# A perceiver kernel on one core: six blocks of the program joined to two, and TensorE multiplies the identity while it waits

## The chip, the cores and the metric

The kernel runs on one core of a Trainium2 chip. A core has TensorE (PE, matmuls; its weight loads are PEld), VectorE (DVE), ScalarE (ACT), GpSimd (POOL) and SyncE (SP, which here only issues transfers). They run side by side and wait for each other through semaphores. The metric is device time in microseconds (us), median of several runs. The kernel before takes 1051.17 us.

## What is computed

A small sequence x of 128 rows of 256 numbers goes through two layers against a context of 12544 rows of 256 numbers. Cut to what matters:

```
# layer 0
x = x + cross_attention(layernorm(x), ctx; 4 heads of 64)        # softmax over 12544 rows
x = x + gated_delta_net(layernorm(x); 12 heads)                  # conv, silu, l2 norms, recurrence, gated norm
x = x + experts(layernorm(x); 8 experts, best 1)
# layer 1
x = layernorm(x) -> x + cross_attention(., ctx; 16 heads of 16)  # softmax over 12544 rows
x = x + gated_linear_attention(layernorm(x))                     # decay scans, sigmoid gate
x = x + experts(layernorm(x); 8 experts, best 2)
```

All matrices are float32, except the keys and queries of the second cross attention, which are split into sums of bf16 parts.

## The kernel before, in words

The program is a row of blocks. A block gives each engine its own list of instructions; between two blocks there is a barrier of all engines, and none starts the next block before every engine has ended the last. `renew` (L80) is such a barrier too, and gives semaphores back. In order of time:

1. **First block** (L298, 0 to 12.5 us): x is loaded and normalised, the queries q0 are made, and the first of 14 pieces (chunks) of the context is loaded and turned by DVE into `ctxT0`. `first_*` are this block's parts in the changed kernel.
2. **Second block** (L368, to 531 us): the loop of the first cross attention over the 14 chunks. In front of the loop stands the chunk-0 work of `PRO0`: keys (`K`, L491), the turned weights (`W`, L498 on PE, L604 and L607 on DVE), scores (`S`), keys and values for layer 1 (`J`, `V`). SP loads the weights that these need at the start of this block.
3. **Gated delta net** (one block, to 636 us), then `renew`.
4. **First experts** (`experts("moe0", ...)`, to 657 us), its own block.
5. **Second cross attention** (to 1008 us), its own block: the norm ln2, the queries, a transfer of the queries out to memory and back (L1571), 17 pairs of score matmuls for a running maximum (L1662, read by DVE at L1780), and the loop over 14 chunks (L1705 scores, L1842 exponentials on ACT, L1718 values).
6. **Linear attention** (to 1032 us), its own block: ln3, six projections (L1984), two scans on DVE, the gate (L1998), the output product (L2005), and between them the turning of the eight experts' weights (L1975).
7. **Last experts** (`experts("moe1", ...)`, to the end), its own block: norm, router (L1342), products of the experts (L1289), the sum weighted by the router on DVE (L1428), the bias.

The norm is a chain over four engines: DVE L139, L141, POOL L149, L151, DVE L144, then PE turns the result (`ln_pe`, L157) and ACT copies it to `hT` (`ln_act`, L162). PE has nothing else to do meanwhile. Each engine runs its list strictly in order, as the code is written. A float32 matmul shows as two records in the trace, a float32 transposition and a bf16 matmul as one.

Of the kernel before, what the change touches and what calls it, by code (L numbers as in the profile page):

```python
# [17 lines left out]
F32 = mybir.dt.float32  # L18
# [6 lines left out]
P = 128  # L25
# [37 lines left out]
E = 8  # L63
# [3 lines left out]
def build(nc, a, out):  # L67
# [47 lines left out]
    with ctx:  # L115
# [182 lines left out]
        with nc.Block() as block:  # L298
            @block.sync
            def _(sp):  # L300
                sp.dma_start(xres[:], a["x"].rearrange("b q d -> (b q) d")).then_inc(S("x_in"), 16)
                sp.dma_start(Wq0[:], wcols(a["L0_xattn_Wq"])).then_inc(S("wq0_in"), 16)
                load_permuted(sp, Wk0[:], a["L0_xattn_Wkv"][:, 0:D], "wk0_in")
                sp.dma_start(mask0[:, 0], mask_rows[:, 0:CH]).then_inc(S("mask0_0"), 16)

            @block.gpsimd
            def _(pool):
                pool.memset(mhalf[:], -0.5).then_inc(S("mhalf"), 1)
                pool.wait_ge(S("mhalf"), 1)
                pool.memset(ident[:], 0.0).then_inc(S("ident"), 1)  # L310
                pool.wait_ge(S("ident"), nth("ident"))
                pool.affine_select(out=ident[:], in_=ident[:], compare_op=ALU.not_equal, fill=1.0, base=0,
                                              pattern=[[-1, P]], channel_multiplier=1).then_inc(S("ident"), 1)
                pool.wait_ge(S("ident"), nth("ident"))
                ln_pool(pool, "ln0")
                pool.memset(acc0[:], 0.0).then_inc(S("acc0"), 1)
                pool.memset(run0[:], LOWEST).then_inc(S("run0_lowest"), 1)
                v = v1s[:].rearrange("p s t w -> p (s t) w")
                pool.memset(v[:, :, 0:H1 * (D1 + 1)].rearrange("p t (h d) -> p t h d", h=H1)[:, :, :, D1],
                            1.0).then_inc(S("v1_ones"), 1)  # L320
                pool.memset(v[:, :, H1 * (D1 + 1):], 0.0).then_inc(S("v1_ones"), 1)

            @block.vector
            def _(dve):
                dve.wait_ge(S("x_in"), 16)
                ln_dve(dve, "ln0")
                for k in range(4):
                    turn_context(dve, k, 0, 0, 0)
                dve.wait_ge(S("q0_psum"), 1)
                dve.tensor_scalar(q0[:].rearrange("p b q -> p (b q)"), bank[1][:, 0:D], S0, None,  # L330
                                  ALU.mult).then_inc(S("q0"), 1)

            @block.tensor
            def _(pe):
                pe.wait_ge(S("ident"), 2)
                ln_pe(pe, "ln0", 0)
                pe.wait_ge(S("ln0_hT"), 1)
                pe.wait_ge(S("wq0_in"), 16)
                for b in range(DC):
                    for k in range(DC):  # L340
                        ins = pe.matmul(bank[1][:, b * P:(b + 1) * P], Wq0[:, k, b * P:(b + 1) * P], hT[:, k, :],
                                        start=(k == 0), stop=(k == DC - 1))
                ins.then_inc(S("q0_psum"), 1)

            @block.scalar
            def _(act):
                load_context(act, 0, 0)
                ln_act(act, "ln0", 0)
# [19 lines left out]
        with nc.Block() as block:  # L368
            @block.gpsimd
            def _(pool):  # L370
                pool.tensor_copy(identb[:], ident[:]).then_inc(S("identb"), 1)
# [54 lines left out]
            def _(sp):  # L426
                def load(c, s):
# [46 lines left out]
            def _(pe):  # L474
                def kv_free(op, c):
# [105 lines left out]
            def _(dve):  # L581
                def side(op, c, s, n):
# [82 lines left out]
            def _(act):  # L665
                def side(op, c, s, n):
# [134 lines left out]
        with nc.Block() as block:  # L801
# [287 lines left out]
            def _(pe):  # L1089
# [51 lines left out]

                pe.wait_ge(S("o0"), 1)
# [118 lines left out]
        def experts(tag, router, router_rows, router_bias, expert_bias, top, last, loads=None, clears=None, turned=None):  # L1261
# [31 lines left out]
            with nc.Block() as block:  # L1293
                @block.sync
# [740 lines left out]
```

## Time and profile before

| | |
|---|---|
| median of 3 runs | 1051.17 us (1048.46 to 1052.52) |
| the profiled execution | 1051.36 us, its span 1049.6 us |
| PE busy | 970.8 us, 92% of the span |
| DVE, ACT, POOL busy | 494.8, 536.3, 301.9 us |
| mean granted clock of TensorE | 0.954 of full |

### The profile page before, as it was taken

The page shows a single profiled execution, that of the slowest core. Times are in us where ns is not written, and L with a number is a line of the kernel's source. Part 1 is how long each engine was busy: PE and PEld are TensorE (multiplying, and loading weights), DVE is VectorE, ACT ScalarE, POOL GpSimd, SP SyncE. Part 2 cuts the span into 40 slices and gives each one's busy share as a digit, 9 for nine tenths or more (in the row PEclk, how much of TensorE's full clock was granted, in tenths as well). Part 3 has the DMA queues.
Part 4 walks back from the last instruction along what each step waited for, and adds up shares of the span by engine and source line. Part 5 has one row for each costly group of instructions (what it writes and reads, how often), then busy time and mean ns, then how long its engine had stood idle before and what let it go on. Part 6 is the DMA issues. An engine that isn't in the chain of part 4 may idle for free. (4 is left out here: it accounts for less than half of the span.)

```text
span 1049.6 us, 21941 instructions
## 1 busy us (share of the span) xinstructions
PE 970.8 (92%) x8332; PEld 582.6 (56%) x8332; DVE 494.8 (47%) x1002; ACT 536.3 (51%) x1250; POOL 301.9 (29%) x424
## 2 busy tenths in 40 slices
PE   6999999999999999999978888589999999999967
PEld 3444544554554445455457875236667666666754
DVE  3224233332423232242245462478778887787434
ACT  1544544454455445455537732126667666666742
POOL 4543353444435344443502710610110000100000
PEclk9999999999999999999979997659999999999987
DMA  6466547535565544443210005676556776566000
GB/s 135 149 176 184 174 171 187 141 141 104 127 182 181 140 128 148 95 124 144 99 46 1 2 2 135 167 192 174 154 148 180 176 191 185 147 164 189 25 1 6
DMA packets 106060, 136.78 MB, mean 130 GB/s; under 512 B 66568, under 2 KB 87840, under 8 KB 103296
## 3 DMA queue, kind: packets, MB, share of 16 engines
q1 hardware_dynamic: 102272, 134.81, 46.5%
q10 hardware_dynamic: 3712, 0.92, 0.6%
q8 instruction: 53, 0.87, 0.3%
q14 instruction: 23, 0.19, 0.1%
HBM read 81.88 MB, written 53.26 MB: 129 GB/s over the span
## 5 line engine op out<-in xcount | busy, mean ns | idle before, releaser
L1780 DVE TENSOR_REDUCE mx<-bank 128x1 f32<-128x896 f32 x224 | 234.1, 1086 | 60.6 <-PE bank L1662 57.6
L1842 ACT ACTIVATE p<-bank 128x512 f32<-128x512 f32 x392 | 204.2, 601 | 105.3 <-PE bank L1705 105.1
L526 PE MATMUL bank<-Wv,ctxT 128*128 128x512 f32 x392 | 183.6, 603 | 0.0
L1662 PE MATMUL bank<-krows,qrows 96*128 96x512 bf16 x448 | 132.0, 379 | 11.2 <-DMA qrows<-qscr 6.7
L1705 PE MATMUL bank<-qrows,krows 99*128 99x128 bf16 x1568 | 125.6, 222 | 5.3 <-ACT p L1842 4.9
L1705 PEld LDWEIGHTS bank<-qrows,krows 99*128 99x128 bf16 x1568 | 100.6, 98 | 42.9 <-issue 10.5
L594 DVE CUSTOM_DVE_ANT_0 sc<-bank,pen 128x448 f32<-128x448 f32 x112 | 65.7, 620 | 102.9 <-issue 102.9
L1718 PE MATMUL bank<-p,v 128*32 128x128 f32 x3136 | 108.5, 277 | 5.1 <-issue 5.1
L413 POOL CAST kt<-kf 128x512 bf16<-128x512 f32 (+1 forms) x56 | 31.2, 558 | 278.4 <-ACT kf L685 278.4
L526 PEld LDWEIGHTS bank<-Wv,ctxT 128*128 128x128 f32 x392 | 70.1, 190 | 72.9 <-issue 68.6
L1718 PEld LDWEIGHTS bank<-p,v 128*32 128x32 f32 x3136 | 80.8, 110 | 39.4 <-ACT p L1842 31.5
L696 ACT COPY v<-bank 128x256 f32<-128x256 f32 x98 | 36.3, 370 | 116.5 <-PE bank L526 116.5
L507 PE MATMUL bank<-ctxT,WTk 128*128 128x512 f32 (+1 forms) x224 | 95.0, 547 | 0.4 <-ACT v1s L697 0.4
L491 PE MATMUL bank<-ctxT,Wk 128*128 128x448 f32 x224 | 90.6, 549 | 3.0 <-PEq L298 3.0
L1601 POOL TENSOR_SCALAR neg<-run 128x16 f32<-128x16 f32 x14 | 3.6, 256 | 271.6 <-DVE run L1795 271.6
L717 ACT COPY pT<-bank 128x512 f32<-128x512 f32 x98 | 56.6, 583 | 47.2 <-PE bank L537 47.1
L709 ACT ACTIVATE sc<-sc,neg 128x448 f32<-128x448 f32 x112 | 73.5, 663 | 0.0
L685 ACT ACTIVATE kf<-bank,b 128x512 f32<-128x512 f32 (+1 forms) x56 | 35.5, 634 | 67.5 <-PE bank L507 67.5
L620 DVE COPY ots<-bank 128x256 f32<-128x256 f32 x14 | 5.9, 425 | 131.4 <-PE bank L549 131.4
L537 PE MATMUL bank<-ident,sc 128*128 128x128 f32 x392 | 62.3, 282 | 4.0 <-ACT pT L717 1.7
L537 PEld LDWEIGHTS bank<-ident,sc 128*128 128x128 f32 x392 | 42.8, 140 | 40.0 <-issue 31.8
L507 PEld LDWEIGHTS bank<-ctxT,WTk 128*128 128x128 f32 x224 | 40.2, 190 | 44.8 <-issue 23.2
(285 smaller groups left out, 1200.7 us busy)
## 6 DMA issues: line engine op xcount, KB each, us to landing
krows<-kscr SPq DMA_DIRECT2D x14, 1536.0 KB, 9.6
krows<-kscr SPq DMA_DIRECT2D x14, 1152.0 KB, 14.3
vscr<-v1s SPq DMA_DIRECT2D x14, 1004.5 KB, 3.9
v<-vscr SPq DMA_DIRECT2D x14, 1004.5 KB, 12.5
ctx<-ctx SPq DMA_DIRECT2D x104, 112.0 KB, 3.6
kscr<-kt SPq DMA_DIRECT2D x14, 768.0 KB, 3.6
kscr<-kt SPq DMA_DIRECT2D x14, 576.0 KB, 3.0
kscr<-kt SPq DMA_DIRECT2D x14, 512.0 KB, 4.5
```

The costliest lines, as they stand in the source:

```text
L491: ins = pe.matmul(bank[kv_bank(op, s)][:, 0:HCH], Wk0[:, i, b * P:(b + 1) * P], ctxT0[:, i, half * HCH:(half + 1) * HCH], start=(i == 0), ...
L507: ins = pe.matmul(bank[kv_bank(op, s)][:, 0:HW[half]], WTk[:, i, b * P:(b + 1) * P], ctxT0[:, i, HO[half]:HO[half] + HW[half]], start=(i = ...
L526: ins = pe.matmul(bank[kv_bank(op, s)][:], ctxT0[:, i, k * P:(k + 1) * P], Wv01[:, i].rearrange("p w o -> p (w o)"), start=(i == 0), stop= ...
L537: ins = pe.transpose(bank[PT[(s + t) % 2]][:, h * P:(h + 1) * P], sc0[:, s, h, t * P:(t + 1) * P], ident[:])
L594: dve.tensor_tensor_reduce(out=sc0[:, s, h, half * HCH:(half + 1) * HCH], in0=bank[SX[k % 2]][:, 0:HCH], in1=pen0[:, half * HCH:(half + 1) ...
L709: act.activation(sc0[:, s, h, cols], sc0[:, s, h, cols], ACT.Exp, bias=neg0[:, h:h + 1], accum_out=den0[:, s, h, half:half + 1]).then_inc( ...
L717: act.copy(pT0[:, t % NPT, :], bank[PT[(s + t) % 2]][:]).then_inc(S("pT0"), 1)
L1662: ins = pe.matmul(bank[b + half][:, 0:HW[half]], qrows[0:KROWS, 0, h, :], krows[half][0:KROWS, r, krow(h), :], start=True, stop=True)
L1705: ins = pe.matmul(bank[ST1[g % 3]][:, i * P:(i + 1) * P], krows[half][:, c % R1, krow(h), cols], qrows[:, c % 2, h, :], start=True, stop=True)
L1718: ins = pe.matmul(bank[OT1][32 * i:32 * i + 32, j * P:(j + 1) * P], v1[:, c % R1, t, h * (D1 + 1):h * (D1 + 1) + 32], p1[:, g % PR, i * P: ...
L1780: dve.tensor_reduce(mx1[:, c % 2, h:h + 1], psum[:, b:b + 2, :].rearrange("p b n -> p (b n)")[:, 0:CH], AX.X, ALU.max).then_inc(S("smread1 ...
L1842: act.activation(p1[:, g % PR, :], bank[ST1[g % 3]][:], ACT.Exp).then_inc(S("exp1"), 1)
```

## The change

**Blocks joined.** The first two blocks become one, and the last four (first experts, second cross attention, linear attention, last experts) become one. Each engine's lists are put one behind the other: `first_tensor(pe)` and then the second block's list, and `moe0[3](pe)`, `second_tensor(pe)`, `linear_tensor(pe)`, `moe1[3](pe)`. Where a barrier had stood for an order between engines, three waits are written: VectorE waits for `run0_lowest` ahead of the first running maximum and for the last rescaling of `acc1` ahead of the linear attention, SP for `ln3_xn` ahead of the last experts' small loads. q0 is made in bank 7 instead of bank 1. The barrier at `renew` and that behind the first attention's loop stay.

**Products of the identity.** A helper `spin(pe, b, n)` multiplies the 128x128 float32 identity with itself n times into a bank that nothing reads. It is called at 20 places, 119 products in all (`spin` counts below), nearly all just ahead of a place where PE waits for a norm, a softmax or a copy.

```diff
+        def spin(pe, b, n):
+            for _ in range(n):
+                pe.matmul(bank[b][:, 0:P], ident[:], ident[:], start=True, stop=True)
...
+        def first_tensor(pe):
+            pe.wait_ge(S("ident"), 2)
+            spin(pe, OT, 9)
+            ln_pe(pe, "ln0", 0)
+            spin(pe, OT, 3)
+            pe.wait_ge(S("ln0_hT"), 1)
...
+            ins.then_inc(S("q0_psum"), 1)
+            spin(pe, OT, 3)
...
                 penalty(0, 0, 0)
+                dve.wait_ge(S("run0_lowest"), 1)
...
+                spin(pe, 5, 5)
                 pe.wait_ge(S("o0"), 1)
...
                 ins.then_inc(S("x1_psum"), 1)
+                spin(pe, 5, 11)
                 ln_pe(pe, "ln1", 7)
+                spin(pe, 5, 2)
                 pe.wait_ge(S("ln1_hT"), 1)
...
                 pe.wait_ge(S("masks"), MASKS)
+                pe.wait_ge(S("qcopy"), 2)
+                spin(pe, 2, 14)
                 pe.wait_ge(S("sq"), 1)
                 norms(ZB[0], 0, "n2k")
-                pe.wait_ge(S("qcopy"), 2)
...
+                spin(pe, 6, 11)
                 for g in range(NG):
                     pe.wait_ge(S("on"), g + 1)
                     heads(g, ZB[g], lambda h: oh[:, h], None, "oT_psum", True)
+                    if g == 0:
+                        spin(pe, 6, 6)
...
+                if last:
+                    pe.wait_ge(S(n("eT")), 5)
+                spin(pe, 3 if last else 7, 6 if last else 3)
+                ln_pe(pe, n("ln"), 0)
+                spin(pe, 3 if last else 7, 2)
...
+            spin(pe, 3, 10)
+            ln_pe(pe, "ln2", 4)
+            spin(pe, 3, 2)
...
+            for n, op in enumerate(PRO1):
+                side(*op)
+            if n >= len(PRO1) - 6:
+                spin(pe, OT1, 2)
...
+        def linear_vector(dve):
+            dve.wait_ge(S("acc1"), 2 * NCH + 1)
...
+        def linear_tensor(pe):
+            spin(pe, 6, 9)
+            ln_pe(pe, "ln3", 0)
+            spin(pe, 6, 2)
...
+            expert(0)
+            expert(1)
+            spin(pe, 6, 7)
+            pe.wait_ge(S("qs"), DC)
...
+            expert(2)
+            expert(3)
+            spin(pe, 6, 10)
+            pe.wait_ge(S("ol"), 1)
...
         with nc.Block() as block:
+            @block.sync
+            def _(sp):
+                moe0[1](sp)
+                second_sync(sp)
+                sp.wait_ge(S("ln3_xn"), 1)
+                moe1[1](sp)
...
+            @block.tensor
+            def _(pe):
+                moe0[3](pe)
+                second_tensor(pe)
+                linear_tensor(pe)
+                moe1[3](pe)
```

The order of instructions at three places, before and now. First PE at the start of the program, before (`ctxT,Wk` are the first keys, L298 and L473 the end of one block and the entry of the next):

```order
L157 MATMUL bank<-ident,xn 128x128 x2
L341 MATMUL bank<-hT,Wq 128x128 x4
L298 UNCONDITIONAL_BRANCH
L473 UNCONDITIONAL_BRANCH
L491 MATMUL bank<-ctxT,Wk 128x448 x8
L498 MATMUL bank<-ident,v 128x128 x4
L518 MATMUL bank<-kT,q 128x448 x2
```

and now:

```order
L163 MATMUL bank<-ident 128x128 x9
L157 MATMUL bank<-ident,xn 128x128 x2
L163 MATMUL bank<-ident 128x128 x3
L343 MATMUL bank<-hT,Wq 128x128 x4
L163 MATMUL bank<-ident 128x128 x3
L496 MATMUL bank<-ctxT,Wk 128x448 x8
L503 MATMUL bank<-ident,v 128x128 x4
L523 MATMUL bank<-kT,q 128x448 x2
L512 MATMUL bank<-ctxT,WTk 128x512 x2
```

The end of the block between the queries (L341, now L343) and the keys is gone, and 15 products stand around the norm and the queries.

Then SP, the queue of transfers, at the same place, before (`v<-` with L_xattn_Wk, Wv and Wq are the weights of layer 1, loaded into the space of `v0`; `Wv` is the weight of the values):

```order
L301 DMA xres<-x 128x256
L302 DMA Wq<-L_xattn_Wq 128x2x256
L296 DMA Wk<-L_xattn_Wkv 32x2x256 x4
L304 DMA mask<-mask_BxSxS_bf 128x896
L298 UNCONDITIONAL_BRANCH
L425 UNCONDITIONAL_BRANCH
L271 DMA v<-L_xattn_Wk 32x8x64 x4
L271 DMA v<-L_xattn_Wv 32x8x64 x4
L450 DMA v<-L_xattn_Wq 128x2x256
L296 DMA Wv<-L_xattn_Wkv 32x2x256 x4
```

and now:

```order
L304 DMA xres<-x 128x256
L305 DMA Wq<-L_xattn_Wq 128x2x256
L301 DMA Wk<-L_xattn_Wkv 32x2x256 x4
L307 DMA mask<-mask_BxSxS_bf 128x896
L276 DMA v<-L_xattn_Wk 32x8x64 x4
L276 DMA v<-L_xattn_Wv 32x8x64 x4
L454 DMA v<-L_xattn_Wq 128x2x256
L301 DMA Wv<-L_xattn_Wkv 32x2x256 x4
```

The weights of layer 1 stand directly behind the mask, without the end of the block between them.

Last PE from the end of the second attention into the linear attention, before (`ident,ots` is the last turn of values, L1984 the projections, L1975 the turned experts' weights, L1991 the divisor, L1998 the gate):

```order
L1679 MATMUL bank<-ident,ots 128x128 x4
L1551 UNCONDITIONAL_BRANCH
L1967 UNCONDITIONAL_BRANCH
L157 MATMUL bank<-ident,xn 128x128 x2
L1984 MATMUL bank<-hT,lT 128x128 x12
L1975 MATMUL bank<-ident,ew 128x128 x8
L1991 MATMUL bank<-qs,blk 128x256
L1975 MATMUL bank<-ident,ew 128x128 x8
L1998 MATMUL bank<-ol,lT 128x128 x4
L1975 MATMUL bank<-ident,ew 128x128 x8
L2005 MATMUL bank<-lT,kvp 128x256 x2
L1975 MATMUL bank<-ident,ew 128x128 x8
```

and now:

```order
L1690 MATMUL bank<-ident,ots 128x128 x4
L163 MATMUL bank<-ident 128x128 x9
L157 MATMUL bank<-ident,xn 128x128 x2
L163 MATMUL bank<-ident 128x128 x2
L1996 MATMUL bank<-hT,lT 128x128 x12
L1985 MATMUL bank<-ident,ew 128x128 x8
L163 MATMUL bank<-ident 128x128 x7
L2004 MATMUL bank<-qs,blk 128x256
L1985 MATMUL bank<-ident,ew 128x128 x8
L163 MATMUL bank<-ident 128x128 x10
L2012 MATMUL bank<-ol,lT 128x128 x4
L1985 MATMUL bank<-ident,ew 128x128 x8
```

Nine products stand in the place of the end of the block, and two, seven and ten more ahead of the three places at which PE waits.

## Rows read from the trace of the kernel before

**Rows 1.** Page, part 2: granted clock in tenths, 40 slices of the span.

```profile
PEclk9999999999999999999979997659999999999987
```

**Rows 2.** Windows: length; busy us (records) of PE, PEld, DVE, ACT, POOL; PEclk; DMA; GB/s.

```profile
1008.00:1010.00 2.00, 0.00 (x0) 0.00 (x0) 1.71 (x5) 0.00 (x0) 0.00 (x0) 1.00 0.03 8
1011.00:1016.90 5.90, 4.89 (x21) 4.49 (x22) 1.22 (x5) 0.37 (x1) 0.00 (x0) 0.50 0.00 0
639.00:648.00 9.00, 7.99 (x26) 5.29 (x26) 2.78 (x13) 4.17 (x8) 1.45 (x5) 0.50 0.59 181
```

**Rows 3.** Timeline: start us, length us, engine, line, operation; first block and after.

```profile
3.62 0.43 SPq L304 DMA_DIRECT2D mask<-mask_BxSxS_bf  x1
...
7.88 2.08 PE L341 MATMUL bank<-hT,Wq 128*128 128x128 f32 x8 [1.31 <-ACT hT L162]
...
11.00 1.17 DVE L285 STREAM_TRANSPOSE ctxT<-ctx 128x448 f32<-128x448 f32 x2 [2.10 <-DMA ctx<-ctx]
...
12.76 1.79 SPq L271 DMA_DIRECT2D v<-L_xattn_Wk  x4
...
12.98 8.16 PE L491 MATMUL bank<-ctxT,Wk 128*128 128x448 f32 x16 [3.02 <-PEq L298]
...
19.81 0.64 DVE L604 STREAM_TRANSPOSE WTk<-v 128x128 f32<-128x128 f32 x2 [6.27 <-DMA v<-L_xattn_Wq]
```

**Rows 4.** Timeline of the steady loop and of the second stage, clock at full.

```profile
46.62 3.17 PE L491 MATMUL bank<-ctxT,Wk 128*128 128x448 f32 x8
...
571.35 1.95 PE L1105 MATMUL bank<-hT,Wc 128*128 128x128 f32 x16
```

**Rows 5.** Timeline of the second stage, first half.

```profile
533.91 2.07 PE L1149 MATMUL bank<-Wo,oT 128*128 128x256 f32 x4 [0.46 <-ACT oT L1020]
...
546.28 5.31 DVE L887 SCALAR_TENSOR_TENSOR cv<-xpad,convw,cv 128x128 f32<-128x128 f32 x18 [0.38 <-ACT cv L978]
...
553.18 1.47 PE L1119 MATMUL bank<-half,sq 128*128 128x2 f32 x12 [1.80 <-DVE sq L896]
```

**Rows 6.** Timeline of the second stage, end.

```profile
628.80 3.10 PE L1138 MATMUL bank<-Wo,oT 128*128 128x256 f32 x8
...
632.17 3.62 PE L1138 MATMUL bank<-Wo,oT 128*128 128x256 f32 x16
```

**Rows 7.** Timeline of the first mixture of experts.

```profile
638.32 1.94 PE L1325 MATMUL bank<-ident,ew 128*128 128x128 f32 x8 [2.53 <-PEq L83]
...
644.85 3.60 PE L1289 MATMUL bank<-eTmoe,hT 128*128 128x512 f32 x4
...
649.16 1.88 PE L1289 MATMUL bank<-eTmoe,hT 128*128 128x512 f32 x4
```

**Rows 8.** Timeline of the second attention, ahead of its loop.

```profile
657.55 0.43 DVE L139 BATCH_NORM_STATS2 stats<-xres 128x6 f32<-128x256 f32 x1 [0.53 <-PEq L1293]
...
660.88 2.07 PE L1728 MATMUL bank<-hT,WTq 128*128 128x128 f32 x8 [0.46 <-ACT hT L162]
...
703.67 1.09 DVE L1780 TENSOR_REDUCE mx<-bank 128x1 f32<-128x896 f32 x1 [2.35 <-PE bank L1662]
```

**Rows 9.** Timeline of the linear attention and the last mixture.

```profile
1011.55 0.69 PE L157 MATMUL bank<-ident,xn 128*128 128x128 f32 x2 [4.26 <-DVE xn L144]
...
1012.70 4.95 PE L1984 MATMUL bank<-hT,lT 128*128 128x128 f32 x24 [0.46 <-ACT hT L162]
...
1024.46 2.08 PE L1998 MATMUL bank<-ol,lT 128*128 128x128 f32 x8 [2.71 <-DVE ol L1932]
...
1028.24 2.08 PE L2005 MATMUL bank<-lT,kvp 128*128 128x256 f32 x4
...
1032.36 0.43 DVE L139 BATCH_NORM_STATS2 stats<-xres 128x6 f32<-128x256 f32 x1 [1.59 <-PEq L1883]
...
1036.64 9.19 PE L1289 MATMUL bank<-eT,hT 128*128 128x512 f32 x16
```

**Rows 10.** Waits of VectorE, 1006 to 1050 us: us, times, longest.

```profile
DVE xres L1428 <- PE bank L1289: 1.8, 3, 0.7
```

More of the change, by code:

```diff
@@ L296, in load_permuted @@
                 sp.dma_start(tile[j * SQ:(j + 1) * SQ], rows[j]).then_inc(S(name), 16)
[L298 to L348, printed above, removed]
@@ L352, in kv_bank, with first_scalar @@
+        def first_scalar(act):
+            load_context(act, 0, 0)
+            ln_act(act, "ln0", 0)
         def kv_bank(op, s):
@@ new lines, in mixture_scalar, with expert @@
+            def mixture_scalar(act):
+                def expert(i):
+                    act.wait_ge(S(n("eT_psum")), i + 1)
+                    act.copy(eT[:, :, i, :], bank[3 + i % 2][:].rearrange("p (k o) -> p k o", k=DC)
+                             ).then_inc(S(n("eT")), 1)
+                if not last:
+                    expert(0)
+                    expert(1)
+                if router_rows:
+                    act.wait_ge(S(n("rwT_psum")), 1)
+                    act.copy(rwT[:].rearrange("p k e -> p (k e)"), bank[1][:, 0:DC * E]).then_inc(S(n("rwT")), 1)
+                ln_act(act, n("ln"), 0)
+                for i in range(2, E):
+                    if not last:
+                        expert(i)
+                    if i == 2:
+                        act.wait_ge(S(n("shifted")), 1)
+                        act.activation(ex[:], lx[:], ACT.Exp).then_inc(S(n("ex")), 1)
+                act.wait_ge(S(n("wtT_psum")), 1)
+                act.copy(wtT[:], bank[1][0:E, 0:P]).then_inc(S(n("wtT")), 1)
@@ L1501, in build @@
         renew(("ew0_in",))
-        experts("moe0", a["L0_ffn_router_w"], True, a["L0_ffn_router_b"], a["L0_ffn_expert_b"], 1, False,
+        moe0 = experts("moe0", a["L0_ffn_router_w"], True, a["L0_ffn_router_b"], a["L0_ffn_expert_b"], 1, False,
                 l1_loads, l1_clears)
@@ L1866, in build @@
+        moe0[0].close()
         l1.close()
@@ new lines, in linear_scalar, with expert @@
+        def linear_scalar(act):
+            def expert(i):
+                act.wait_ge(S("moe1eT_psum"), i + 1)
+                act.copy(eT1[:, :, i, :], bank[EB[i % 4]][:].rearrange("p (k o) -> p k o", k=DC)).then_inc(S("moe1eT"), 1)
+            ln_act(act, "ln3", 0)
+            act.wait_ge(S("ng"), 1)
+            act.activation(ng[:], ng[:], ACT.Exp).then_inc(S("eng"), 1)
+            act.wait_ge(S("qkv_psum"), 2)
+            act.copy(qkv[:, 4:6], bank[4][:, 0:D].rearrange("p (c t) -> p c t", c=2)).then_inc(S("vl"), 1)
+            expert(0)
+            expert(1)
+            act.activation(spare[:], bg[:, 0:1], ACT.Sigmoid)
+            expert(2)
+            act.wait_ge(S("gate_psum"), 1)
+            for c in range(DC):
+                act.activation(gl[:, c], bank[6][:, c * P:(c + 1) * P], ACT.Sigmoid,
+                               bias=bg[:, c:c + 1]).then_inc(S("gate"), 1)
+            for i in range(3, E):
+                expert(i)
@@ L1884, in _ @@
+        moe1 = experts("moe1", a["L1_ffn_Wg"], False, a["L1_ffn_bg"], a["L1_ffn_be"], 2, True, turned=eT1)
+        with nc.Block() as block:
+            @block.sync
[4 more added lines that the diff above has]
+                moe1[1](sp)
             @block.gpsimd
             def _(pool):
-                ln_pool(pool, "ln3")
+                moe0[2](pool)
+                second_gpsimd(pool)
+                linear_gpsimd(pool)
+                moe1[2](pool)
+            @block.tensor
[4 more added lines that the diff above has]
+                moe1[3](pe)
+            @block.scalar
+            def _(act):
+                moe0[4](act)
+                second_scalar(act)
+                linear_scalar(act)
+                moe1[4](act)
@@ L2010, in build @@
-        experts("moe1", a["L1_ffn_Wg"], False, a["L1_ffn_bg"], a["L1_ffn_be"], 2, True, turned=eT1)
+                moe0[5](dve)
+                second_vector(dve)
+                linear_vector(dve)
+                moe1[5](dve)
+        moe1[0].close()
         la.close()
```

1024 lines of the change are left out of this document (501 added, 523 removed).

## The prediction, made before the changed kernel was run

> **What bounds the kernel now.** I read the page first. PE is busy in nearly the whole span, but the slices of the granted clock are not all 9: there are dips behind the middle and at the end [rows 1]. So I cut the span at the stages and asked for the granted clock of short windows. It has two levels, 1.00 (2.4 GHz) and 0.50 (1.2 GHz). From 1008 to 1010 us PE has no record and the clock is still 1.00; from 1011 to 1016.9 us it works through at 0.50; from 639 to 648 us likewise [rows 2]. Each fall comes behind a stretch in which PE did little, and the work behind the wait pays for it. The timelines of the small stages then show what ends each wait. These stages are one chain over four engines; every microsecond saved on it is a microsecond of the kernel, and the two loops only move forward.
>
> **The unit.** At full clock 16 records of 128 columns take 1.95 us [rows 4], 0.12 each. At 0.50, 8 records take 2.08 us [rows 9]; 8 at full would take 8 x 0.12 + 0.1 for the end = 1.07. So 1024 columns of float32 records cost 1.0 us more at the low level. In the first block the clock column reads full, but the 8 records of the queries took the same 2.08 us [rows 3], so I take them as low. A product of the identity is two such records: 0.24 us at full, 0.5 at low.
>
> **Start.** Before, the queries end at 7.88 + 2.08 = 9.96, and the keys start at 12.98 because the block has to end; they take 8.16 us [rows 3] where the same 16 records take 2 x 3.17 = 6.34 in the loop [rows 4]. The first half of the context is turned long before, the second at 11.00 + 1.17 = 12.17 [rows 3]. Now nine products fill PE until the norm comes, three the copy, so that the queries or at the latest the keys run at full clock: queries until 8.9, three products until 9.7, the first half of the keys until 12.8, later than 12.17, the rest until 16.0. Before it was 21.14: 5.1 us earlier at best. The next work needs the turned weights of layer 1, whose transfers were issued from 12.76 and awaited until 19.81. SP now issues them behind the mask, from 3.62 + 0.43 = 4.05, 8.7 us earlier [rows 3]; they have 16.0 - (19.81 - 8.7) = 4.9 us of slack to share the engines with the context. I take 4.3, since the first products run low and may be 0.4 us too long at two places. Bounds: 5.1 above; below, 1.0, the queries' clock alone, if sharing costs the transfers all that the earlier issue gives.
>
> The Trainium skill (DMA: Bandwidth & Descriptors, Issuing engines are not separate DMA queues) says that transfers from different engines run on the same 16 DMA engines and interleave. By that rule the weights on SP's queue delay the context on ACT's, which this trace cannot show, since before nothing followed the mask on SP. It is the third rival below.
>
> **Delta net, first half.** Five products stand ahead of the turn of o0, eleven in the norm, two at the copy. They keep the clock: the output product of 4 records of 256 columns goes from 2.07 to 1.05 [rows 5], the two turns save 0.2 each, the gate projection (4 records) about 0.5. These 1.9 us reach VectorE's chain to R. Behind R the convolutions waited 0.38 us more for ACT's taps, which waited for PE [rows 5]; at full clock PE is early, so this goes too. Sum 2.3. Bounds 1.0 (the clock falls once) and 2.5. Fourteen products (3.4 us) stand ahead of the norms, where PE waited 1.80 us [rows 5]. They fit because PE's projections ahead of them also end over a microsecond sooner. At low clock they would not.
>
> **Delta net, end.** Eleven and six products stand in the waits of the gated norm. 8 records of 256 columns took 3.10 us, while 16 of the same took 3.62 [rows 6], that is 1.8 for 8. Saved 1.3, and 0.3 for the turns between: 1.6. Bounds 0 and 1.8.
>
> **First experts.** The barrier ahead of it stays (PE idle 2.53 us), and the clock is at 0.50 until 648 [rows 2, 7]. Three products in front of the norm's turn and two behind it do not fit: PE had idle gaps of about 1 us there together, five low products take 2.5. Against these 1.5 us lost stand an earlier rise, as PE now works without gaps from the start: the next turned experts save 0.9 (8 records: 1.94 low [rows 7], 1.04 at full), the first product 3.60 - 1.88 = 1.7 [rows 7]. Then ACT's exponential, which stands in its queue between two experts' copies, holds some of it back. I take 1.2. Bounds -1.5 and 2.6.
>
> **Into the second attention.** The barrier costs VectorE 0.53 us [rows 8]; it goes. Ten products (2.4 us) lie in the norm. The query projection saves 1.0 (2.07 for 8 records [rows 8]), the turn 0.2. Sum 1.7; bounds 0.3 and 2.0. From here to the loop VectorE's maxima set the pace, but behind them PE is waited for (2.35 us ahead of one maximum [rows 8]) at the low clock: the two products at the end of this prologue, called once, lie bare and cost 2 x 0.5 = 1.0.
>
> **Linear attention and last experts.** PE waited 4.26 us for ln3; nine products fill half of this, and I take it that the clock holds. Of the 24 records of the projections [rows 9] VectorE waits for the first 16: 2.0 us saved. The divisor's wait is not on the path. Gate 8 records: 1.0. Output product, the same columns in 4 records: 1.0. The barrier ahead of the last experts cost 1.59 us [rows 9], because PE and ACT still turned experts; it goes, and the turns are hidden behind the norm. The two norms' turns save 0.2 each. The 16 records of 512 columns took 9.19 us [rows 9] and would take 16 x 0.44 = 7.1 at the rate of rows 7, but VectorE's additions waited only 1.8 us for them [rows 10], so 1.8. The joint at 1008 us is worth 0.3 at most, taken in full. Sum 2.0 + 1.0 + 1.0 + 1.6 + 0.4 + 1.8 + 0.3 = 8.1. Bounds 3.5 (the clock falls twice) and 8.6. PE's added wait for five copied experts holds up only products and the norm's turn, due 2.7 us later.
>
> **Sum.** 4.3 + 2.3 + 1.6 + 1.2 + 1.7 - 1.0 + 8.1 = 18.2. Products a little too long: 0.1 at some ten places, -1.0 (0 to 2). 17.2 off the profiled execution's 1051.36 (span 1049.6 and 1.8 around it) is 1034.2; the median is 0.2 lower, so 1034.0. POOL, ACT and VectorE get their second lists earlier in the first block; nothing waits for these. The three new waits are for things long done.
>
> **The rivals.**
> - *The clock holds only in part.* For it: nine products end 2 us before the norm does, and PE goes low after little work. The tail then loses 2 to 3 us, the delta net 1 to 2, the first experts their 1.2: 1034.0 + 5.5 = 1039.5.
> - *The products do not keep the clock at all, but fit.* Against it: ordinary matmuls without gaps did raise it. Left are the joints (0.5 + 1.6 + 0.3), about 3.0 of the start, -1.0 and -1.0: 3.4, so 1047.8, within the bound of no change.
> - *The transfers collide.* The weights pass beside the context on the DMA engines, and its second half comes over 3 us later: the start is worth 1.0 instead of 4.3, and the time is 1037.3.
> - *Slower: the products run low and are then twice as long.* Place: all waits outside the first block, 104 products, each 0.26 us longer than what fits: 27 us, less about 5 of slack, less 5.4 from joints and start: 1051 + 16 = 1067. It decides once about a third of the places are entered low. Against it: products without a gap are themselves the work behind which the clock rose in every stage before.
> - *No effect,* because a barrier's cost moves to the added waits: against it speaks that each awaited event is over when the waiting engine arrives.
>
> **How the numbers follow.** A measurement of this kernel tells 0.5% (5 us) from no change. Forecast (1029.5 to 1037) 0.62; clock in part 0.20; transfers collide 0.08; only joints 0.06; slower 0.04. So faster 0.90, no change 0.06, slower 0.04. The range reaches from all upper bounds but a little (22 us saved) to the clock held in part at its bad end, 9 us saved: 1029 to 1042.5.
>
> **What would show it.** Right: granted clock 1.00 from 532 us on through the delta net's first projections, again behind ln3 and through the last products, which then take about 7 us; the first keys start near 9.7 us; no barrier row ahead of the norms of the last three stages; VectorE's additions at the end wait for nothing. The prologue of the second attention still at 0.50. Wrong: windows at 0.50 behind the products; PE's turn of a norm starting visibly later than `xn` is ready, which would say that the products are too long; the context landing past 13 us.

## The result, and the profile after

| | median | ratio to before, 95% | mean granted clock |
|---|---|---|---|
| before, beside it | 1050.29 us (4 runs) | | 0.954 |
| changed | 1037.14 us (1033.1 to 1038.46, 4 runs) | 0.9868 [0.9838, 0.9899] | 0.975 |

Foretold were 1034.0 us, in 1029 to 1042.5. The profiled execution took 1038.27 us (span 1036.5), 13.1 less than that of before. The sum of the forecast was 17.2. The page shows where the clock is still low, against [rows 1]:

```profile
PEclk9999999999999999999999999659999999999999
```

Of the dips, the one in the 26th and 27th slice is left; those of the 21st and 25th slice (about 530 to 550 and around 640 us before) and the one at the end are gone. Windows of the changed kernel (columns as in [rows 2]):

```profile
532.00:548.00 16.00, 15.15 (x117) 13.13 (x117) 10.04 (x32) 10.48 (x22) 0.65 (x4) 1.00 0.00 1
548.00:552.00 4.00, 4.00 (x27) 2.83 (x24) 2.55 (x6) 3.63 (x13) 0.00 (x0) 0.57 0.01 2
...
585.00:590.00 5.00, 5.00 (x32) 5.00 (x32) 1.52 (x3) 2.95 (x12) 1.89 (x2) 0.66 0.00 0
631.00:648.00 17.00, 14.98 (x78) 9.78 (x79) 8.10 (x25) 6.57 (x13) 1.75 (x13) 1.00 0.72 190
658.00:701.00 43.00, 29.46 (x121) 9.71 (x121) 27.44 (x27) 4.51 (x10) 16.58 (x11) 0.50 0.69 172
...
1008.00:1017.00 9.00, 8.44 (x72) 7.96 (x70) 6.62 (x13) 3.94 (x7) 0.00 (x0) 1.00 0.02 3
1017.00:1036.00 19.00, 14.62 (x69) 9.28 (x69) 10.77 (x36) 5.26 (x11) 0.80 (x2) 1.00 0.02 7
```

The stretches at 532, 631 and behind 1008 us run at 2.4 GHz; 43 us ahead of the second loop stay at 1.2 GHz, and a few microseconds at 548 and at 585 us fell too. Now the rows that answer to [rows 3], [rows 5 to 9], in order of time:

```profile
7.79 1.16 PE L343 MATMUL bank<-hT,Wq 128*128 128x128 f32 x8 [0.75 <-ACT hT L167]
9.46 3.17 PE L496 MATMUL bank<-ctxT,Wk 128*128 128x448 f32 x8
12.11 1.17 DVE L290 STREAM_TRANSPOSE ctxT<-ctx 128x448 f32<-128x448 f32 x2 [3.06 <-DMA ctx<-ctx]
14.34 0.64 DVE L610 STREAM_TRANSPOSE WTk<-v 128x128 f32<-128x128 f32 x2 [0.22 <-DMA v<-L_xattn_Wq]
...
539.42 5.31 DVE L895 SCALAR_TENSOR_TENSOR cv<-xpad,convw,cv 128x128 f32<-128x128 f32 x18
550.03 4.48 PE L1120 MATMUL bank<-Wg,hT 128*128 128x512 f32 x8
623.07 1.89 PE L1146 MATMUL bank<-Wo,oT 128*128 128x256 f32 x8
631.39 1.06 PE L1336 MATMUL bank<-ident,ew 128*128 128x128 f32 x8 [2.54 <-PEq L83]
636.79 1.88 PE L1304 MATMUL bank<-eTmoe,hT 128*128 128x512 f32 x4
650.65 1.16 PE L1741 MATMUL bank<-hT,WTq 128*128 128x128 f32 x8
...
1006.35 0.44 PE L157 MATMUL bank<-ident,xn 128*128 128x128 f32 x2 [1.97 <-DVE xn L144]
1007.25 2.95 PE L1996 MATMUL bank<-hT,lT 128*128 128x128 f32 x24
1017.29 1.16 PE L2012 MATMUL bank<-ol,lT 128*128 128x128 f32 x8 [0.49 <-DVE ol L1944]
1020.15 1.13 PE L2019 MATMUL bank<-lT,kvp 128*128 128x256 f32 x4 [0.83 <-DVE kvp L1952]
1025.35 7.11 PE L1304 MATMUL bank<-eT,hT 128*128 128x512 f32 x16
```

Read the length behind the start: 8 records of 128 columns take 1.06 to 1.16 us where they took 1.94 to 2.08, and the last products 7.11 us instead of 9.19. The first keys start at 9.46, not 12.98. The second half of the context came 1.1 us later than before, at 12.11 instead of 11.00, and the keys behind it started at once (PE had stood idle 0.75 us ahead of them).

The loss stands at one place, the transfer of the second attention's queries to memory and back. SP's timeline before, and then the transfers issued from 630 to 666 us (KB each, median us to landing):

```profile
644.34 3.11 SPq L1478 DMA_DIRECT2D v<-vscr  x1
...
665.33 0.38 SPq L1567 DMA_DIRECT2D qscr<-q  x1
```

```profile
v<-vscr SPq DMA_DIRECT2D x1, 1004.5 KB, 20.5
...
qscr<-q SPq DMA_DIRECT2D x1, 192.0 KB, 2.3
```

The same two views of the changed kernel:

```profile
637.42 3.60 SPq L1493 DMA_DIRECT2D v<-vscr  x1
...
654.19 0.38 SPq L1580 DMA_DIRECT2D qscr<-q  x1
...
661.01 2.78 SPq L1584 DMA_DIRECT2D qrows<-qscr  x6
```

```profile
v<-vscr SPq DMA_DIRECT2D x1, 1004.5 KB, 23.0
...
qscr<-q SPq DMA_DIRECT2D x1, 192.0 KB, 6.8
```

Before, the values of chunk 0 landed at 644.34 + 20.5 = 664.8 us, and the query write was issued 0.5 us behind that and landed in 2.3 us. In the changed kernel they land at 637.42 + 23.0 = 660.4, while the write is issued at 654.2, 6.2 us ahead of that; it landed 0.6 us behind them, and only then could the reads start. The chain had become 11.1 us shorter, the loads that begin behind `renew` started only 7 us earlier.

By stage, of the two profiled executions:

| stage | foretold | measured |
|---|---|---|
| start, to the end of the first loop | 4.3 | 4.5 |
| delta net, first half | 2.3 | 2.3, and 1.55 given back behind 548 us |
| delta net, end | 1.6 | 1.6 |
| first experts | 1.2 | 2.55 |
| joint and queries of the second attention | 1.7 | 0.5 + 1.2 |
| query round trip | none | -4.5 |
| two bare products | -1.0 | -0.85 |
| second loop | 0 | -0.85 |
| linear attention and last experts | 8.1 | 8.2 |
| products too long | -1.0 | 0 seen |
| sum | 17.2 | 13.1 |

The 0.85 us of the second loop has no cause shown. From the first score to the last turn of its values PE takes 333.4 to 335.6 us in the six profiles that go into it low, as before, and have no further fall in it: 333.6 before, 335.3 and 335.6 in the changed kernel's two profiles, but also 335.6 with the joints alone.

### The profile page after: what moved, and what is told of

Same layout as the page of the kernel before. It is cut to its first block and busy times, and to the rows that moved or that the text cites. A ratio compares the mean times of both kernels' runs of the same rounds, so it can differ in the third digit from the quotient of the medians.

```text
span 1036.5 us, 22370 instructions
## 1 busy us (share of the span) xinstructions
PE 979.1 (94%) x8570; PEld 596.9 (58%) x8570; DVE 494.4 (48%) x1002; ACT 535.5 (52%) x1250; POOL 301.3 (29%) x424
```

## The experiments

My theory: joints and clock pay about as foretold, and what is missing went into the query write, which is held behind chunk 0's loads. Rivals: that write is slow for its own form; the products or the joints alone are the gain; the clock's falls at 548 us come from where the products stand.

### Joints alone, products alone

```diff
         def spin(pe, b, n):
-            for _ in range(n):
-                pe.matmul(bank[b][:, 0:P], ident[:], ident[:], start=True, stop=True)
+            return
```

> The changed kernel without any product of the identity; all joints of blocks stay. My theory: the joints give what the profiles show at them: the first block's end about 3.0 us at the first keys (which then run at the low clock), the joint ahead of the second attention's norm 0.5, the joint ahead of the last experts 1.6 and at 1008 us 0.3, less up to 4.5 if the query write of the second attention waits behind chunk 0's loads here as well (it is issued earlier by less, so less of it): 2 to 5 us saved, so 1045 to 1048 us. Granted clock 0.50 in the tail (1001 to 1010 us), additions waiting for PE again, last products about 9.2 us. Rival A (products alone do nothing, the joints are the whole gain): about 1037 us. Rival B (the joints cost what they give): 1050 us.

The other one has the blocks of before and all groups of products:

```diff
@@ before
+                spin(pe, OT, 9)
                 ln_pe(pe, "ln0", 0)
+                spin(pe, OT, 3)
...
+                pe.wait_ge(S("qcopy"), 2)
+                spin(pe, 2, 14)
                 pe.wait_ge(S("sq"), 1)
                 norms(ZB[0], 0, "n2k")
-                pe.wait_ge(S("qcopy"), 2)
```

> The kernel before with its blocks and barriers, and all twenty-odd groups of products put in at their places. My theory: the products give the clock's part: start 1.0 to 2.0 (keys behind the barrier perhaps low again), delta net front 2.3 less 1.6, delta net end 1.6, first experts 2.5, queries 1.2, less 0.9 for the two bare ones, tail about 5.5 to 6, of which up to 4.5 is lost again at the query write. About 1040 to 1043 us, and together with the joints-only kernel (1045 to 1048) the two gains should add up to the whole change's 13 us within about 2. Rival (products are too long and only the joints pay): 1050 us or more.

Measured beside before at 1052.22 us: joints alone 1044.84 us, 0.9917 [0.9894, 0.994]; products alone 1041.44 us, 0.9901 [0.9876, 0.9926]. The first came out 0.2 us under what I expected (1045 to 1048), the second inside it. By the ratios they give 0.83% and 0.99%, 1.8 together, where the whole change gives 1.3 (1.4 in the comparison further below). Each part gains by itself beyond its interval, so both rivals that give one part the whole gain fall (that the products alone give less than the whole is only just outside the intervals). And something seems to be given back when both act: the query write took 2.3 us in the joints' profile, 5.3 in the products', 6.8 in the changed kernel's. The joints' profile in the tail:

```profile
1009.00:1017.00 8.00, 4.58 (x22) 4.18 (x23) 2.33 (x9) 0.37 (x1) 1.10 (x10) 0.57 0.04 5
1023.00:1031.00 8.00, 4.04 (x28) 3.41 (x28) 4.00 (x9) 3.15 (x7) 0.80 (x2) 1.00 0.00 0
1033.00:1038.00 5.00, 5.00 (x9) 2.10 (x9) 4.12 (x21) 0.88 (x2) 0.00 (x0) 0.66 0.00 0
```

Without products the clock falls at 1009 us as before. At 1023 us it did not fall again, with no product there and behind the same wait as before (2.72 us for 2.71):

```profile
1024.77 1.16 PE L2011 MATMUL bank<-ol,lT 128*128 128x128 f32 x8 [2.72 <-DVE ol L1943]
```

So the gate and the output product ran at full clock here (1.16 and 1.13 us, 2.08 each before), 1.9 us that no joint explains and that the products would give as well. In the first block the division is sharp. The profile of the joints, then that of the products:

```profile
9.88 7.74 PE L495 MATMUL bank<-ctxT,Wk 128*128 128x448 f32 x16
...
17.45 0.60 PE L502 MATMUL bank<-ident,v 128*128 128x128 f32 x4
```

```profile
13.22 7.92 PE L499 MATMUL bank<-ctxT,Wk 128*128 128x448 f32 x16 [3.08 <-PEq L303]
...
20.98 0.60 PE L506 MATMUL bank<-ident,v 128*128 128x128 f32 x4
```

The turn of the weights starts at 20.98 us before, 16.46 after. Of these 4.5 us the joint gives 3.5 and the products give nothing without it: the queries do run at full clock (1.16 us), but the barrier waits for VectorE's turn of the second half of the context (11.27 + 1.17 us) and the copy of q, and behind PE's 3.08 us in it the keys start at the low clock again (before, they took 8.16 us there, though the clock column reads 1.00):

```profile
13.20:17.00 3.80, 3.78 (x6) 1.97 (x7) 0.62 (x1) 0.42 (x1) 3.25 (x9) 0.55 0.45 102
```

Together with the joint they give the last microsecond.

### The query write

```diff
             gather(sp, 0, 0)
             gather(sp, 0, 1)
-            fetch_values(sp, 0)
...
             sp.dma_start(qrows[0:KROWS, 1], qrows[0:KROWS, 0]).then_inc(S("qrows_copy"), 16)
+            fetch_values(sp, 0)
             gather(sp, 1, 0)
```

> The changed kernel with one move on SyncE's queue: the values of the second attention's chunk 0 (1004.5 KB) are fetched behind the queries' write, reads and copy instead of ahead of them. My theory: in the changed kernel the query write (issued 654.2 us) landed only after 6.8 us because chunk 0's transfers still filled the DMA engines until about 660; with 1 MB less ahead of it the engines are through about 5 us sooner, the write lands in about 2.3 us and the first scores start up to 4.5 us earlier: total 1033 to 1035 us. Rival A (the round trip is late because of its own form, many small pieces, and not because of what is ahead): no change, 1037 us. Rival B: the values are now late for the loop's first products with them, and the gain is given back: wait on the values ahead of chunk 0's products, 1037 us or more.

In the next one the write and the six reads are issued by ScalarE:

```diff
-            sp.dma_start(qscr..., q3[...]).then_inc(S("qscr"), 16)
-            sp.wait_ge(S("qscr"), 16)
-            for j in range(NJ):
-                sp.dma_start(qrows[j * D1:(j + 1) * D1, 0], qscr[...]).then_inc(S("qrows_in"), 16)
+            act.dma_start(qscr..., q3[...]).then_inc(S("qscr"), 16)
+            act.wait_ge(S("qscr"), 16)
+            for j in range(NJ):
+                act.dma_start(qrows[j * D1:(j + 1) * D1, 0], qscr[...]).then_inc(S("qrows_in"), 16)
```

> The changed kernel with the query write and its six reads issued by ScalarE instead of SyncE; chunk 0's loads stay ahead in time on SyncE's queue. If the write is held because it stands behind the loads in one queue (first in, first out), it lands in 2 to 3 us and the time is 1033 to 1035 us. If it is held because all transfers share the same 16 DMA engines, it still lands only when they are through, or in part: 4 to 7 us, and the time is 1035 to 1038 us. I expect something between, nearer the first: 1034.5 us.

Measured: 1036.28 us, 0.9856 [0.984, 0.9873], and 1037.83 us, 0.9856 [0.9834, 0.9878]. Neither can be told from the changed kernel, and both lie above what I expected (1033 to 1035, and 1034.5). Their profiles tell more. ScalarE as the issuer:

```profile
qscr<-q ACTq DMA_DIRECT2D x1, 192.0 KB, 4.2
```

The write's landing against that of the last of chunk 0's loads, in us of each profile (issue and time to landing added):

| profile | last load landed | write issued | write landed |
|---|---|---|---|
| before | 664.8 | 665.3 | 667.6 |
| joints alone | 665.7 | 664.0 | 666.3 |
| products alone | 664.0 | 659.3 | 664.6 |
| changed | 660.4 | 654.2 | 661.0 |
| changed, again | 659.4 | 654.7 | 659.9 |
| write issued by ScalarE | 659.2 | 655.6 | 659.8 |
| products doubled (below) | 665.1 | 662.4 | 665.7 |
| warm prologue alone (below) | 659.7 | 655.2 | 660.3 |

With nothing ahead the write takes 2.3 us. With the joints alone it takes the same, so there it was not held. In the other six it is issued 2.7 to 6.2 us ahead of the loads' landing and lands 0.5 to 0.6 us behind them, whoever issues it. So the write's own form is not what was slow, and the queue isn't either, against my leaning: moving it to ScalarE changed nothing but the hour of issue. The Trainium skill (DMA: Bandwidth & Descriptors, Issuing engines are not separate DMA queues) says that transfers of all issuers run on the same 16 DMA engines and interleave, and that a second issuer saves only the time of issuing. The numbers agree on the saving (the split further below: 1.36 us of issuing for 2.78); but the small write did not come through early in any of these profiles, it landed behind the megabytes from either engine.

With the values moved away the write landed in 3.0 us (still 0.5 us behind the last key load, which had landed at 655.1), and the first score came 8.0 us behind the write's issue instead of 12.2. But the megabyte now stood ahead of the keys of chunk 1 in SP's list, and PE waited for these, the rival with keys for values:

```profile
680.31 0.91 PE L1673 MATMUL bank<-krows,qrows 96*128 96x512 bf16 x2 [2.91 <-DMA krows<-kscr]
```

### The changed kernel again, and its products doubled

> The changed kernel once more, unaltered, to see which of its spells at the low clock come again and which do not. In the five profiles so far with the products or joints, the long low spell from the query wait to the start of the second loop came every time (37 to 44 us), while short ones of 3.4 us came at other places each time: at 548 or 552 in two of four with the products, at 585 to 595 in every profile but one, and in one profile each at 522, 985, 765 and 771 us. My theory: the fall at 548 us is not a fault of the products' place but one of these passing ones, so it is absent here about as often as not, and each such spell moves the time by up to 1.7 us; the runs lie between 1032 and 1040 us, median 1036. Rival: the fall at 548 comes back at the same place, so it belongs to the change.

```diff
-            for _ in range(n):
+            for _ in range(2 * n):
```

> The changed kernel with every group of products twice as long. This is the test of the rival that I held for the slower side: that the counts are too large. Outside the first block 104 products are added at 0.24 us each at full clock, 25 us; the slack behind the present counts is at most 5 us in the profile, so the time is 1037 + 15 to 22 us: 1052 to 1059 us, about as slow as the kernel before. If the waits had much more room than I read, it stays under 1042 us. If longer filling also prevents the short low spells, the granted clock's mean rises from 0.977 to 0.985 and gives back 2 to 3 us.

Measured beside before at 1052.7 us: again 1037.07 us, 0.9859 [0.984, 0.9877]; doubled 1044.91 us, 0.9933 [0.9917, 0.995].

The fall at 548 us did not come again. It came at 548 or 552 us in three of the ten profiles with the single products (the changed kernel, products alone, warm and split), and with the joints alone, without any product, at 552, so it is not fixed by the place of the products. One around 585 to 590 us came in nine of them, as at 590 us before; four had one at 631 to 640 us, behind `renew`; others came in the loops, where PE is busy nearly throughout: two each at 522 and 765 us, one each at 771 and 986. None of these is without an idle stretch of PE. Ahead of 522 us PE waits 1.41 us at the last softmax of the first loop, ahead of 585 us 1.35 us and then has only 12 records of 2 columns, ahead of 986 us it waited 1.21 us, and its records have a gap of 1.7 to 2.0 us ahead of those at 765 and 771:

```profile
520.93 1.19 PE L542 MATMUL bank<-ident,sc 128*128 128x128 f32 x8 [1.41 <-ACT sc L717]
```

That wait of 1.41 us stands in all ten, and the clock fell behind it in two. Behind `ln3` it fell in four, in spite of the products there, as in the profile with ScalarE as issuer:

```profile
1010.00:1015.00 5.00, 4.99 (x30) 4.79 (x29) 0.84 (x3) 0.37 (x1) 0.00 (x0) 0.66 0.05 4
```

So the products make falls rarer, not impossible. Executions of one kernel differ by 2 to 8 us, of which the falls are a part only: with ScalarE as issuer 1035.1 us came at a mean clock of 0.979 and 1043.4 at 0.970, but the changed kernel took 1033.1 at 0.978 and 1038.5 at 0.977.

With twice the products it fell nowhere from 532 to 1042 us but ahead of the second loop:

```profile
532.00:666.00 134.00, 122.18 (x968) 109.13 (x966) 61.81 (x132) 64.15 (x163) 37.39 (x44) 1.00 0.16 42
666.00:701.00 35.00, 24.84 (x69) 6.75 (x69) 25.26 (x25) 1.02 (x4) 16.81 (x11) 0.51 0.70 180
701.00:1042.00 341.00, 325.12 (x5404) 235.48 (x5402) 245.04 (x298) 214.74 (x436) 26.52 (x104) 1.00 0.53 137
```

It cost 7.8 us, not the 15 to 22 I expected: of 25 us of added products up to two thirds found room. My 5 us of slack were much too small, though part of the 17 us is not slack: the absent falls gave back some, and of 7.7 us by which the query write was issued later than in the run again, the loads ahead of it hid 1.9 (it landed 5.8 later). Ahead of the first turn at the delta net's end the room is nearly used up by the single counts (0.17 us idle).

### The prologue kept warm, and the order of the transfers

The last five begin from the two things left: 43 us at the low clock, and the order of SP's loads. The edit that keeps PE busy ahead of the second loop, put on top of the kernel with the values moved:

```diff
-            pe.wait_ge(S("qrows_in"), 16 * NJ)
             pe.wait_ge(S("lT"), len(LB))
-            for n, op in enumerate(PRO1):
-                side(*op)
-            if n >= len(PRO1) - 6:
-                spin(pe, OT1, 2)
+            spin(pe, OT1, 28)
+            pe.wait_ge(S("qrows_in"), 16 * NJ)
+            for op in PRO1:
+                side(*op)
+                if op[0] == "S":
+                    spin(pe, OT1, 2)
```

> The kernel with the values of chunk 0 fetched behind the queries, and the second attention's prologue kept busy: 28 products of the identity in the wait for the query rows, two behind each of the prologue's scores, and the two bare ones at its end gone. My theory: PE waits for VectorE's maxima anyway (it is busy 0.9 of each 1.06 us at the low clock, 0.45 at full), so products there cost nothing at full clock, and the second loop then begins at full clock instead of 7.6 us later: 3 to 4 us from that, 0.9 from the two bare products: about 1032 us, 4 to 5 us under the changed kernel run beside it. Rival A: the prologue is bound by VectorE and the first steps of the loop by other engines, so the clock there is worth under 1 us. Rival B: the wait for the rows is entered low and the products are then too long (0.5 us each): the prologue starts up to 5 us late and the kernel is slower than the changed one.

In the next one, besides, ScalarE issues the reads 1, 3 and 5 of the six (`act.dma_start` behind a wait for `qscr`), SP the reads 0, 2 and 4.

> As the kernel with the warm prologue, and of the six reads that spread the queries over the rows three are issued by ScalarE instead of SyncE. The six issues take 2.77 us one after the other on SyncE; on two engines 1.4. My theory: the last read is issued 1.4 us sooner and lands about that much sooner, so 0.5 to 1.4 us under the kernel with the warm prologue, about 1031 us. Rival: the landing is set by the transfers and not by the issue; then no difference, and ScalarE's added issues cost nothing either since it waits there.

Measured: 1034.5 us, 0.9832 [0.981, 0.9854]; split 1035.31 us, 0.9847 [0.9824, 0.987]. The mean clock went to 0.993. The gain of 2.6 us on the changed kernel run again is smaller than expected (the intervals overlap), and one row of the first profile says why:

```profile
682.48 0.90 PE L1673 MATMUL bank<-krows,qrows 96*128 96x512 bf16 x2 [4.57 <-DMA krows<-kscr]
```

What was won waits for the late keys of chunk 1. The split gave nothing that can be measured: its issues take 1.36 instead of 2.78 us, but the reads took longer to land (3.3 and 3.8 us instead of 3.0), and the first score came 0.6 us sooner behind the write's issue (7.9 for 8.5). The rival, that the transfers set the landing, holds for most of it.

So the values have to go behind the keys of chunk 1 as well:

```diff
@@ l1_loads
-            fetch_values(sp, 0)
@@ second_sync
             gather(sp, 1, 0)
             gather(sp, 1, 1)
+            fetch_values(sp, 0)
             fetch_values(sp, 1)
```

> As the kernel with the values of chunk 0 fetched later, but behind the keys of chunk 1 too, not ahead of them. In that kernel the query write did land in 3.0 us and the first score came 4.2 us sooner relative to its query, but then PE waited 2.91 us for the key rows of chunk 1, because the moved megabyte stood ahead of them in SyncE's queue. My theory: in this order both waits go, since the values are wanted only about 30 us after the copy of the query rows and the keys of chunk 1 about 16 us after it: 3.5 to 4.5 us under the changed kernel (1037.1 in the last comparison), 1032.5 to 1033.5 us, and no wait for key rows at the seventeenth score. Rival: the values now come late for the loop's first products with them, and the gain is lost there.

> The changed kernel with its transfers where they are, and only the prologue kept busy by products (28 in the wait for the rows, two behind each score, the bare two gone). Separates the clock's share from that of the transfers. My theory: the loop begins at full clock, worth 1.5 to 3 us, and the two bare products 0.9: 1033 to 1034.5 us; the part of the wait that 28 products do not fill (about 5 us) may let the clock fall once at the prologue's start, without cost, since VectorE sets the pace there. Rival: with the late query write the prologue stays low, the pairs of products behind the scores are then 1.06 us each where 0.2 are free, and the prologue is up to 15 us longer.

> Both together: values of chunk 0 behind the keys of chunk 1, and the prologue kept busy. In the kernel that had the values ahead of those keys and the busy prologue PE waited 4.57 us for the keys at 682 us, and the clock fell there. My theory: both the wait and the fall go; 4.5 us from that wait and up to 1.5 from the clock, off 1034.5: 1028.5 to 1030.5 us, the fastest of all here, and granted clock 1.00 from the first score to the loop. Rival: VectorE's maxima and the transfers bound the prologue whatever the clock, and it is no faster than the better of the two parts alone (1033).

Measured beside before at 1051.79 us:

| | median | ratio, 95% |
|---|---|---|
| order of transfers alone | 1033.3 us | 0.9834 [0.9808, 0.9859] |
| warm prologue alone | 1036.59 us | 0.986 [0.9834, 0.9886] |
| both | 1030.09 us | 0.9791 [0.9768, 0.9814] |

The order alone, in its profile: the write lands in 2.3 us, the first score starts 7.6 us behind its issue (12.2 in the changed kernel), and no wait for key rows stands among PE's waits of 655 to 700 us (us, times, longest):

```profile
PE bank L1673 <- DMA qrows<-qscr: 7.8, 1, 7.8
PE bank L1673 <- DVE mx L1794: 2.8, 11, 0.5
PE bank L1681 <- POOL n L1625: 1.7, 1, 1.7
```

That is the 4.5 us of the table back. The median is 3.8 under those of the changed kernel, which ran in other comparisons, and inside what I expected; by the ratios it is 0.25 to 0.35%, and the intervals overlap, so that the times alone do not prove the gain.

The warm prologue alone missed what I expected. Its wait for the rows is longer than 28 products, and the clock fell behind it:

```profile
666.00:671.00 5.00, 5.00 (x26) 4.06 (x26) 4.06 (x4) 0.00 (x0) 5.00 (x1) 0.66 0.94 249
...
765.00:770.00 5.00, 4.61 (x52) 3.50 (x55) 2.20 (x3) 2.17 (x4) 0.00 (x0) 0.66 0.97 236
```

While it was low, a score with its two products took 1.6 us where VectorE needs 1.06, so the rival was right in small; and it fell once more in the loop. With both edits, the prologue is at 1.00 but for one fall at 680 us, behind PE's short waits for VectorE and POOL at the running maximum:

```profile
654.00:680.00 26.00, 23.03 (x158) 17.83 (x157) 17.12 (x18) 0.00 (x0) 19.24 (x11) 1.00 0.76 207
680.00:685.00 5.00, 4.74 (x23) 3.80 (x24) 3.14 (x4) 0.38 (x2) 0.20 (x1) 0.66 0.48 147
685.00:700.00 15.00, 14.20 (x199) 9.74 (x198) 11.58 (x12) 8.16 (x16) 0.00 (x0) 1.00 0.89 236
```

The first score to the linear attention's norm takes 334.9 us, against 337.9 with the order alone. This kernel is the fastest of all, 2.1% under before and by the ratios 0.7% under the changed one, with intervals that do not overlap.

## Why the prediction was right or wrong

**Start.** Right: 4.5 for 4.3, as the joint 3.5 and the clock of queries and keys 1.0. The lower bound, the queries' clock with weights that come late, was not tested; with the barrier in place that clock gave 0.

**Transfers collide** (a rival). The mechanism exists and was small here: the context came 1.1 us late, not 3.

**Delta net.** Both sizes right (2.3, 1.6). "They keep the clock" was too strong for the rest of the first half: the fall at 548 us cost 1.55 us in this execution, which left 0.75 net, below the bound of 1.0; it is absent in seven of the ten profiles, the changed kernel's second among them.

**First experts.** Undersized in this execution: 2.55 for 1.2. I let the clock stay at 0.50 until 648 us, since the barrier is not joined. It was at 1.00 behind the same wait of 2.54 us, here and in five others of the ten profiles; in four it fell at 631 to 640 us, for one short stretch instead of three. Before, PE went into that barrier after a low stretch of its own (627 to 632 us); now the work ahead of it runs at full clock, which may be why, though no run tests it alone. With the fall the stage gave less: in the changed kernel's second profile it took 16.3 us from its first turned expert to the product of its bias, against 17.5 before and 14.9 here, a gain of 1.15. That 1.2 fits this one is luck: the term took the clock for low from the start.

**Into the second attention.** Here the prediction failed. The 1.7 us were right (0.5 + 1.2), and also that the two bare products cost 0.85. But the step said that from there to the loop only the maxima and the clock count. It left out the query write, which stands behind chunk 0's loads. These start behind `renew`, 7 us earlier, and the chain arrives 11 us earlier; the step asked where the engines were, never where the queue was. It cost 4.5 us. The order of transfers alone brings it back in its profile, and with it the kernel takes 1033.3 us, where 1034.0 was forecast. That the rest adds up to the forecast is partly luck: the first experts and the products too long came out 2.35 us better than forecast, the fall at 548 us and the second loop 2.4 worse.

**Linear attention and last experts.** Right: 8.2 for 8.1, with each row as foretold (1.16, 1.13, 7.11 us; additions that wait for nothing). But that the clock holds there is not assured: it fell behind `ln3` in four of ten profiles. In three of them the stretch from this norm's turn to the last one took 19.0 to 19.2 us instead of 17.6; in the fourth, products alone, the fall was over when the projections began (2.94 us) and cost nothing there.

**Products too long.** Wrong in its favour: nothing seen, and even doubled counts cost only 7.8 us net. The slack of 5 us, with which the slower rival was priced, was far too small (up to 17 were found).

**What stays open.** Joints and products together give about half a percent less than their parts. The query write explains 1.5 us of these five in the profiles (it is late by 0 and 3.0 us alone, 4.5 together); in the joints' profile the clock held by itself at 1023 us, 1.9 us that are counted in both parts; one profile does not say how often, and the intervals are too wide to place the rest. Why the clock falls near 585 us in nine of ten profiles, behind a wait of 1.35 us, and at 522 us in two, behind one of 1.41 us, was not tried.

## What to carry to other kernels

When a chain of small steps gets shorter, list the large transfers that its small ones will now meet: a 192 KB write that came half a microsecond behind them lands with the last of them if it is issued earlier, from whatever queue, and the remedy is to start less ahead of it, and to put what is moved behind all that is wanted sooner. Filling PE's waits pays at the next stretch of work on the path. Across a barrier it may or may not (the clock held behind 2.54 us in six of ten profiles, but the keys behind 3.08 us started low with the products alone). One profile shows one outcome of the clock: take the falls of several executions before one is laid to the code.

## What the runs showed of the hardware

- The granted clock falls to 0.50 also behind idle stretches of PE as short as 1.2 to 2.0 us, mostly for some 3.5 us (771 us: 7.5), and not each time: behind 1.35 us in nine of ten profiles (585 us), behind 1.41 us in two (522 us). A fall that reached the projections behind `ln3` cost 1.4 to 1.6 us.
- A wait of 2.54 us with nothing on PE left the clock at 1.00 in six of ten profiles; in the kernel before the same wait was followed by 9 us at 0.50 [rows 2, 7].
- A transfer of 192 KB issued 2.7 to 6.2 us ahead of the landing of the last of three loads (3.7 MB in all) landed 0.5 to 0.6 us behind it in six profiles, from either issuing engine; issued behind them or 1.7 us ahead it took 2.3 us.
- Two products between two bf16 score matmuls cost nothing at full clock while VectorE set the pace, and its sixteen maxima went from 1.06 to 1.00 us apiece (16.9 to 16.1 us in three profiles).
